# Splitting the normalised images: ACT writes them in fp32 and GpSimd makes the fp16 halves, where DVE made one of them

## The reference, cut to what matters

```python
# x: (8, 512, 128, 128)
x = x + _L0_conv_ref(_gn(x), ...)              # attention over all pixels, in 8 heads of 64 channels
x = x + _L1_conv_ref(_gn(x), bias, up_filter, down_filter)

def _gn(v, G=32, eps=1e-5):                    # groups of 16 channels
    ...
    return ((g - m) / jnp.sqrt(s + eps)).reshape(v.shape)

def _L1_conv_ref(x, bias, up_filter, down_filter):
    y = _upfirdn2d_sep(x, up_filter, UP, 1, PADDING, float(UP * UP))     # twice the size, 12 taps
    y = y + bias[None, :, None, None]
    y = jnp.where(y >= 0, y, y * SLOPE) * GAIN
    y = jnp.clip(y, -CLAMP, CLAMP)
    return _upfirdn2d_sep(y, down_filter, 1, DOWN, (0, 0, 0, 0), 1.0)    # half the size again
```

## Time and profile before

| what | value |
|---|---|
| median of 3 runs | 19641.44 us |
| profiled execution, its own time | 19647.12 us |
| its span (first to last instruction) | 19645.4 us |
| PE busy | 17717.4 us (90%) |
| DVE busy | 13859.5 us (71%) |
| ACT busy | 9606.8 us (49%) |
| POOL busy | 4847.5 us (25%) |
| granted clock of PE, mean | 0.941 |

### The profile page before, as it was taken

How to read it: one execution, slowest core, us unless ns; L and a number is a source line. 1 busy time by engine, 2 the same in 40 slices (tenths; PEclk the granted TensorE clock), 3 DMA queues, 4 the chain that set the end, 5 groups by cost and what they waited for, 6 DMA issues and landing times.

```text
span 19645.4 us, 433534 instructions
## 1 busy us (share of the span) xinstructions
PE 17717.4 (90%) x140128; PEld 13270.6 (68%) x140128; DVE 13859.5 (71%) x26939; ACT 9606.8 (49%) x18080; POOL 4847.5 (25%) x9749
## 2 busy tenths in 40 slices
PE   7898988989889898898988989889898898988988
PEld 5676666776667766677666776667766677766776
DVE  6667766677666776667766677666776667766677
ACT  3455544555445554455544555445554454544545
POOL 1122211222122222222221222212222222321223
PEclk9999999999999999999999999999999999999999
DMA  1111111111111111111111111111111111111110
GB/s 62 42 35 52 42 37 42 35 52 42 39 40 35 52 43 38 40 35 52 44 39 38 35 52 44 39 39 34 52 46 38 38 34 52 46 39 39 31 52 18
DMA packets 1090897, 817.33 MB, mean 42 GB/s; under 512 B 24900, under 2 KB 1073476, under 8 KB 1073604
## 3 DMA queue, kind: packets, MB, share of 16 engines
q1 hardware_dynamic: 1089988, 805.81, 13.1%
HBM read 537.30 MB, written 268.44 MB: 41 GB/s over the span
## 4 chain that ended last, share of the span: by engine, by line
PE 77%; DVE 10%; ACT 6%; issue 6%; DVEq 1%; ACTq 0%; SPq 0%; POOL 0%; DMA 0%; POOLq 0%
PE ps L752 74%; ACT yb L448 5%; DVE t L671 3%; DVE sth L642 3%; PE ps L789 2%; DVE yb L711 1%; DVE xh L621 0%; ACT xn L429 0%; ACT t L426 0%; DVE xn L666 0%; DVEq L686 0%; ACTq L448 0%; DVE mrun L575 0%; DVE pt L617 0%; DVEq L684 0%
## 5 line engine op out<-in xcount | busy, mean ns | idle before, releaser
L448 ACT ACTIVATE yb<-ps,bias_b 128x532 f32<-128x532 f32 x4096 | 2880.8, 703 | 3378.4 <-PE ps L752 3246.9
L752 PE MATMUL ps<-dn_t,yb 128*128 128x64 f32 (+1 forms) x32768 | 4368.5, 270 | 23.7 <-POOL yb L365 21.6
L752 PEld LDWEIGHTS ps<-dn_t,yb 128*128 128x128 f32 x32768 | 4094.8, 191 | 129.3 <-issue 26.0
L365 POOL TENSOR_SCALAR yb<-yb 128x512 f32<-128x512 f32 x4096 | 2521.0, 615 | 5502.9 <-DVE yb L711 5500.2
L711 DVE SCALAR_TENSOR_TENSOR yb<-yb 128x532 f32<-128x532 f32 x4096 | 2911.2, 711 | 1245.7 <-ACT yb L448 1221.3
L752 PE MATMUL ps<-up,t 128*128 128x266 f16 x24576 | 3501.3, 278 | 0.0
L752 PE MATMUL ps<-up,xn 128*128 128x266 f16 x12288 | 2188.0, 288 | 570.9 <-DVE t L671 286.1
L752 PEld LDWEIGHTS ps<-xh,pt 128*128 128x128 f32 x8192 | 1677.8, 207 | 1327.1 <-issue 1167.0
L752 PEld LDWEIGHTS ps<-up,t 128*128 128x128 f16 x24576 | 2355.9, 103 | 303.3
L355 POOL COPY tspr<-tmax 128x512 bf16<-128x512 bf16 x1024 | 627.9, 613 | 7716.8 <-DVE tmax L627 7716.8
L752 PE MATMUL ps<-xh,pt 128*128 (+1 forms) x8192 | 1983.5, 397 | 52.4 <-DVE mrun L575 52.4
(11 more groups left out here) (142 smaller groups left out, 23446.1 us busy)
## 6 DMA issues: line engine op xcount, KB each, us to landing
xc<-in_x SPq DMA_DIRECT2D x128, 2048.0 KB, 13.8
xh<-in_x SPq DMA_DIRECT2D x512, 512.0 KB, 4.6
out<-xh SPq DMA_DIRECT2D x512, 512.0 KB, 3.5
bias_b<-in_bias SPq DMA_DIRECT2D x1, 256.0 KB
bias_r<-in_bias SPq DMA_DIRECT2D x10, 2.0 KB
wa<-in_WaT SPq DMA_DIRECT2D x2, 16.0 KB
wb<-in_WbT SPq DMA_DIRECT2D x2, 16.0 KB
wv<-in_WvT SPq DMA_DIRECT2D x2, 16.0 KB
```

The lines of the kernel that those rows point to most:

```text
L365: nc.gpsimd.tensor_scalar(v[:, :, 0:2 * P], v[:, :, 0:2 * P], CLAMP, -CLAMP, ALU.min, ALU.max).then_inc(s_yc, 1)
L448: act.activation(yb[:, i % YRING, :, :], y_ps[i % 2], ACT.Identity, scale=UPGAIN * GAIN, bias=bias_b[:, bass.ds(c0 + i, 1)]).then_inc(s_y, 1)
L752: return nc.tensor.matmul(o, l, r, start=start, stop=stop, skip_group_check=share)
```

## The change

ACT's instruction now writes the normalised batch in fp32 into `xn` (`norm`, in the place of `xn_high`). POOL makes the high half by a copy from fp32 to fp16 and the low half by a `tensor_tensor` subtraction (`xn_split`). DVE's `norm` and `norm_low` are gone. In the loop POOL does the split of batch j+2 in batch j ahead of the clip of image 4; since `xn` has one buffer, ACT waits for the split of the batch before (`s_xn`) ahead of each `norm`, ahead of the loop too.

```diff
+            def xn_split(g, par):
+                wait_alone(pool, s_xs, g + 1)
+                nc.gpsimd.tensor_copy(xn_2[:, par, 0, :, :], xn[:]).then_inc(s_xnh, 1)
+                wait_alone(pool, s_xnh, g + 1)
+                nc.gpsimd.tensor_tensor(xn_2[:, par, 1, :, :], xn[:], xn_2[:, par, 0, :, :],
+                                        ALU.subtract).then_inc(s_xn, 1)
...
+                    if more and i == 4:
+                        xn_split(g + 2, par)
...
-                with pool.Fori(0, NBAT // 2) as j:
-                    clip_rows(NBAT * u + 2 * j, 0)
-                    clip_rows(NBAT * u + 2 * j + 1, 1)
+                for par in range(2):
+                    xn_split(NBAT * u + par, par)
+                with pool.Fori(0, NBAT // 2 - 1) as q:
+                    for par in range(2):
+                        clip_rows(NBAT * u + 2 * q + par, par, True)
+                for par in range(2):
+                    clip_rows(NBAT * (u + 1) - 2 + par, par, False)
...
-                def xn_high(j, par, gr):
-                    act.activation(xn_2[:, par, 0, :, :], xh[:, bass.ts(j, IMG), :], ACT.Identity,
-                                   scale=r1[:, bass.ds(gr, 1)], bias=nmr1[:, bass.ds(gr, 1)]).then_inc(s_xnh, 1)
+                def norm(j, gr):
+                    act.activation(xn[:], xh[:, bass.ts(j, IMG), :], ACT.Identity,
+                                   scale=r1[:, bass.ds(gr, 1)], bias=nmr1[:, bass.ds(gr, 1)]).then_inc(s_xs, 1)
...
                         if i == LAG and after(2):
-                            xn_high(j + 2, par, (j + 2) // 2)
+                            act.wait_ge(s_xn, NBAT * u + j + 2)
+                            norm(j + 2, (j + 2) // 2)
...
-                xn_high(0, 0, 0)
-                xn_high(1, 1, 0)
+                norm(0, 0)
+                act.wait_ge(s_xn, NBAT * u + 1)
+                norm(1, 0)
...
-                def norm(j, gr):
-                    nc.vector.tensor_scalar(xn[:], xh[:, bass.ts(j, IMG), :], m1[:, bass.ds(gr, 1)],
-                                            r1[:, bass.ds(gr, 1)], ALU.subtract, ALU.mult).then_inc(s_xs, 1)
-
-                def norm_low(j, par):
...
-                for j in range(2):
-                    if j:
-                        wait_alone(dve, s_xn, NBAT * u + 1)
-                    norm(j, 0)
-                    norm_low(j, j)
...
-                        if after(2) and i == 2:
-                            norm(j + 2, (j + 2) // 2)
-                        if after(2) and i == 3:
-                            norm_low(j + 2, par)
```

More of the change, by code:

```diff
@@ L357, in _, with clip_rows @@
             pool.sem_inc(s_yq, YRING)
-            def clip_rows(g, par):
+            def xn_split(g, par):
[4 more added lines that the diff above has]
+                                        ALU.subtract).then_inc(s_xn, 1)
+            def clip_rows(g, par, more):
                 wait_alone(pool, s_t1, IMG * (g + 1))
```

## The result

The changed kernel takes 20111.33 us, median of four runs (20084.46 to 20168.25), beside 19641.53 us (19640.77 to 19642.05) of the kernel before. The ratio is 1.0243, interval 1.0221 to 1.0265: slower by 470 us where 68 were forecast, and outside the range. The profiled execution took 20114.67 us.

A forecast was written before the change was run, and what follows sets the result against it. PE, busy 90% of the span, was taken as the bound, with DVE and POOL counting only where PE waits. 50 us ahead of the loop plus 18 in first batches made 68, so about 19710 us (+0.35%), range 19645 to 19900.

The forecast's parts named there:

- DVE's relief is worth nothing in the loop: In the batch loop, the work leaving DVE ran under DVE's own idle time, so removing it gains 0 us.
- The prices of the two instructions: On POOL, for 1024 elements, the copy would take 1.03 us and the two-input subtraction 2.0 us.
- Ahead of the loop and first batches: PE starts later ahead of the loop, net 50 us over 32 units; port waits in units' first batches add 18 us.
- The step that failed: In steady batches, POOL needs some 0.08 us lead, so image 4's leaky relu goes before the subtraction; cost 0.
- rival 1: In steady batches the subtraction takes the port first, leaky relu 1.84 us late: 765 us, about 20475 in all; chance 0.12.
- The rest of the port: In steady batches, image 5's leaky relu starts 0.26 us late behind the subtraction, reads near 1.0 us, and costs 0.

The follow-up runs named there:

- the later subtraction: The changed kernel with a small POOL memset between copy and subtraction, so the subtraction comes later: 19725.88 us, ratio 1.0040.
- only the loop changed: The changed kernel with ACT and DVE making a unit's first two batches as before, POOL splitting only batches 2 to 15: 19918.15 us, ratio 1.0129.
- the sooner subtraction: The changed kernel with the split put ahead of the 20-column copy of image 3, so the subtraction comes sooner: 21141.57 us, ratio 1.0760.
- The kernels with two and four `bn_stats`: The kernel before, with two or four unused statistics instructions on DVE behind norm_low: 20071.55 us (ratio 1.0215) and 21376.39 us (1.0881).

## Why the prediction was wrong

**DVE's relief is worth nothing in the loop: right.** Free batches take 19.14 us in the trace of the changed kernel, and all 416 do with the later subtraction, where DVE has none of the removed work.

**The prices of the two instructions: nearly right.** The copy took 1.036 us for 1.03, the subtraction 2.12 for 2.0. The Trainium skill's figure for 2048 elements (GPSIMD Engine Reference, "Elementwise — side-by-side cycle accounting") had given an estimate of 2.25. The trace lies in the middle between the two.

**Ahead of the loop and first batches: right in kind.** 54 us for 50, because the subtraction took 0.12 us longer and the hand-over between POOL's two instructions there 0.26 us instead of 0.19; 15 us for 18 (by the prediction's own terms, 0.85 less 0.26, the slip is 0.59 and not 0.55 us, which is 19 us).

**The step that failed** is the lead that POOL was said to need: "How far ahead POOL must be to win, one row bounds: with a lead of 0.11 it did; I assume some 0.08, so the leaky relu goes first, to 6650.52." The row bounds the lead from above only, and the 0.08 near it was assumed. Two rows had already a smaller one: the clip starts at 6647.86 and norm_low at 6647.93, and norm_low reads 1.62 instead of 1.23 us, so POOL won with 0.07. In the trace before, this is so for all 448 norm_low of the loop, with leads of 69 to 74 ns. The runs show that 6 ns are enough (in 74 of 74 batches of the changed kernel, in 53 of 57 with only the loop changed). The working itself had the two arrivals at 6649.80 and 6649.81, POOL 10 ns ahead. With the right lead it would have said that the batch is undecided or POOL's, and not the leaky relu's. The distance of 10 ns is in part luck, since the copy's rate came from two shapes; measured, it scatters from 3 ns behind to 14 ns ahead, so both outcomes occur in one run. The forecast and rival 1 were not two cases to choose between but two ends of a mixture. The later subtraction (0 of 416 held) and the sooner one (416 of 416) show both ends.

**Rival 1 was mis-sized.** It counted 1.84 us a batch, the wait alone, and put the clock at nothing without a reason. A held batch costs 203 + 186 = 389 us over 98, or 3.97 us, since PE's stop of 2 us is mostly followed by 3.4 or 6.8 us at half clock. By the rival's own count of 416 batches that gives 20475; the kernel with the sooner subtraction took 21141.57. The kernels with two and four `bn_stats` show that the clock is what makes the difference.

**The rest of the port was right.** The leaky relu of image 5 reads 1.10 us in free batches (near 1.0 expected), and costs nothing. The Trainium skill's rule (SBUF — State Buffer, "SBUF: two separate sides"), that the shared ports are locked for a whole instruction by whoever starts first, agrees but for 0.14 us: subtraction and leaky relu read 2.12 and 2.69 us in held batches, 2.70 and 0.71 in free ones, so the leaky relu got through 0.14 us before the subtraction's recorded end. It says nothing of starts as close as these.

**Open.** Why ACT's or POOL's instruction is some nanoseconds early or late in a given batch, and so why j = 1 is held in 31 units and those from j = 3 on in one of six, the runs don't settle; the stamps say only that POOL's mean lead is 8.5 ns at j = 1 and 2 to 4 ns later on. Nor do they show what makes 23 of the 98 held batches keep the full clock.

## What to carry to other kernels

Before work with two inputs goes to GpSimd, take from the trace when the DVE instruction that shares its ports arrives, and look at the distance between the two starts. When it is smaller than what the times scatter by, neither order can be counted on: price both, or move one of them. With the later subtraction the starts lay 44 to 57 ns apart, and the order was the same in all 416 batches. And a wait that stops TensorE for some 2 us is to be priced with the stretch at half clock behind it, which here about doubled it.

## What the runs showed of the hardware

- A lead of some 6 ns decides who has the ports shared by DVE and GpSimd. With the subtraction 6 to 14 ns ahead the leaky relu was held in 74 of 74 batches of the changed kernel, at 5 ns in 24 of 61, at 4 ns or less in none of 281. With only the loop changed it was held at 6 ns in 53 of 57 and at 5 ns in none of 10. The loser's recorded duration holds its wait.
- A subtraction of 1024 fp32 elements a partition into fp16 takes 2.12 us on GpSimd, the copy to fp16 1.036 us, and the second starts 0.185 us after the first when it waits for it in the loop.
- A stop of TensorE of 2.09 us was followed by the 1.2 GHz level in 75 of 98 cases, for 3.4 or 6.8 us; a stop of 1.65 us in 22 of 32, one of 0.96 us in none of 416.
- An extra instruction on GpSimd (0.12 us) in each batch of the loop made a kernel 385 us faster.
